# A decoder layer on one core: cross-attention queries of six of eight head groups as seven block products for eight

## The chip, the cores and the metric

One core of a Trainium2 chip runs the whole kernel. The metric is the time of one execution on the device, in microseconds (us); a kernel is run several times and the median is given. A profiled execution is one further run with the hardware profiler on; its span reaches from the first to the last instruction.

## The reference

One post-norm decoder layer in float32, on 8 sequences of 128 tokens with 512 features: x = LN(x + SelfAttention(x)); x = LN(x + CrossAttention(x, ctx)); x = LN(x + FeedForward(x)). What matters here is the cross-attention:

```
q = (query @ wq), 32 heads of 128, rotated by position     k, v = key @ wk, value @ wv, 8 heads of 128
rotate(t) = t * cos + concat(-t[64:], t[:64]) * sin
out = softmax(q k^T / sqrt(128) + mask) v,  heads 4g to 4g+3 use key head g;   result = out @ wo
```

wq is 512 x 4096. With the tokens of all sequences side by side, a head's query tile is a 128 x 1024 product with a contraction of 512.

## The kernel before, in words

Every matmul operand is split into an upper and a lower half (fp32r), and a product is three passes of them: `product`, line 31, whose matmuls all carry line L35. The program is a chain of four classes: ProjectSelf, AttendSelf, AttendCross (prefix C_ in the rows), FeedForward (D_). Each engine's instructions are written out by hand in one order, and semaphores are waited for one by one; an instruction that waits holds up all behind it on its engine.

AttendCross works through 64 steps, step n for head group n // 8 and sequence n % 8, plus three steps to drain. In a step (`decoder_layer`, from line 1750) TensorE does, in this order: the transposes of the probabilities of step n - 2 (`transpose`, L1096), the scores of step n (`scores`, L1114), the output product of step n - 3 (`outputs`, twelve matmuls with wo), the values of step n - 2 (`values`, three matmuls with C_pT), and one query tile (`queries`, `project`), twelve matmuls: four chunks of the contraction by three passes, 128 features of one head by 512 tokens. Five tiles ahead of their use, one a step, until step 58.

VectorE in a step (`vector`, from L1217): the reciprocal of step n - 1's sums (L1190); the rotation of a query tile (`rotate`, L1165 to L1167: the cosine on 128 partitions, the sine on two halves of 64, as the halves change places), read from the PSUM bank of the product; the lower half of the transposed probabilities of step n - 2 (`turned_lo`, L1196), which the value products wait for; the masked row minima (L1180); the residual (L1228); the lower half of the head outputs (`output_lo`, L1203).

ScalarE: upper half of the transposes (L1046), upper half of the outputs (L1055, waits for the values), four exponentials (L1035), and the upper half of one piece of weights (`Ring.hi`, L166). GpSimd (`gpsimd`, from L1244): softmax scaling of step n - 1 (L1249), which waits for the reciprocal; the rotation's sum (`tile_sum`, L1242); the lower half of one piece of weights (`Ring.lo`, L171), which waits for ScalarE's.

Weights come in pieces of 128 x 512 through a ring of five slots (`Ring`, line 140); a load waits until the piece five before it is split. SP issues all DMAs, in order: in `AttendCross.sync` (L1006) the pieces, and between them the keys and values of a whole group (1.5 MB, two buffers). Scores and transposes have two PSUM banks each, the query products two.

Of the kernel before, what the change touches and what calls it, by code (L numbers as in the profile page):

```python
# [5 lines left out]
F32 = mybir.dt.float32  # L6
F32R = mybir.dt.float32r
# [4 lines left out]
P = 128  # L12
# [11 lines left out]
KV = 3 * NT  # L24
# [432 lines left out]
class AttendSelf:  # L457
# [80 lines left out]
    def sync(self, eng):  # L538
# [3 lines left out]
        for n in range(self.STEPS):  # L542
# [29 lines left out]
            if n == self.NS + 1:  # L572
# [4 lines left out]
                self.cross.load_kv(eng, 0)  # L577
# [353 lines left out]
class AttendCross:  # L931
# [3 lines left out]

    Q = HG
# [5 lines left out]
    STEPS = NS + 3  # L942

    def __init__(self, chip, before, x1, trig, rows, ring, first, kv_d, dram):
# [7 lines left out]
        self.kv = [pool(f"kv{i}", (36, 16)[i], [P, KV], F32R) for i in range(2)]  # L952
        self.q = [pool(f"q{half}", 104 + 8 * half, [P, self.Q, HALF]) for half in range(2)]
# [21 lines left out]

    def query(self, r):

        return by_batch(self.q[r // self.Q % 2][:, r % self.Q, :])

    def split(self, n):  # L980


        piece = 2 * self.Q * (n // B + 1) + n % B - 1
        return piece if 2 * self.Q <= piece < self.PIECES else None

    def target(self, i):

        g, j = i // (2 * self.Q), i % (2 * self.Q)
        return [t[:, :] for t in (self.w[j] if j < self.Q else self.wo[g % 2][j - self.Q])]


    def load_piece(self, eng, i):

        src = self.dram["wq" if i % (2 * self.Q) < self.Q else "wo"][i // (2 * self.Q), :, i % self.Q, :]
        self.ring.load(eng, self.first + i, src)

    def load_kv(self, eng, g):

        wait(eng, self.s_pv, B * (g - 1))
        eng.dma_start(self.kv[g % 2][:, :].bitcast(F32), self.kv_d[g]).then_inc(self.s_kv[g % 2], 16)  # L1000
# [5 lines left out]
    def sync(self, eng):  # L1006
# [5 lines left out]
        self.load_kv(eng, 1)  # L1012
# [845 lines left out]
```

## Time and profile before

| | |
|---|---|
| median of 3 runs (881.39 to 882.78) | 881.53 us |
| the profiled execution | 884.05 us |
| its span | 881.9 us |
| TensorE clock granted over the span | 0.997 of full |

A row of a view with lines reads: line, engine, operation, output<-inputs by the program's names, count, then busy time, mean of one, idle time before. A row in order of time reads: start, duration, engine, line, operation, count, and in brackets the idle time before it and what ended it. PE is TensorE's matmul queue, PEld its weight loads, DVE is VectorE, ACT ScalarE, POOL GpSimd.

### The profile page before, as it was taken

The page shows a single profiled execution, that of the slowest core. Times are in us where ns is not written, and L with a number is a line of the kernel's source. Part 1 is how long each engine was busy: PE and PEld are TensorE (multiplying, and loading weights), DVE is VectorE, ACT ScalarE, POOL GpSimd, SP SyncE. Part 2 cuts the span into 40 slices and gives each one's busy share as a digit, 9 for nine tenths or more (in the row PEclk, how much of TensorE's full clock was granted, in tenths as well). Part 3 has the DMA queues.
Part 4 walks back from the last instruction along what each step waited for, and adds up shares of the span by engine and source line. Part 5 has one row for each costly group of instructions (what it writes and reads, how often), then busy time and mean ns, then how long its engine had stood idle before and what let it go on. Part 6 is the DMA issues. An engine that isn't in the chain of part 4 may idle for free.

```text
span 881.9 us, 15308 instructions
## 1 busy us (share of the span) xinstructions
PE 855.9 (97%) x4748; PEld 708.9 (80%) x4748; DVE 604.5 (69%) x2030; ACT 425.8 (48%) x1424; POOL 455.0 (52%) x406
## 2 busy tenths in 40 slices
PE   7999899999999999999999999999999999999996
PEld 6787788788877788888888888888888887778884
DVE  5466688788877676766766666666666767545646
ACT  5336877777771544444444444444444446341320
POOL 4726766766675544444444444444444578545102
PEclk9999999999999999999999999999999999999998
DMA  8679987876864111211212112013131123000001
GB/s 294 261 218 202 217 187 162 182 152 153 162 206 177 37 36 37 108 37 65 80 36 108 37 34 102 34 37 108 37 107 37 49 69 100 13 25 25 25 1 48
DMA packets 68368, 88.23 MB, mean 100 GB/s; under 512 B 7232, under 2 KB 44352, under 8 KB 67264
## 3 DMA queue, kind: packets, MB, share of 16 engines
q1 hardware_dynamic: 68288, 87.26, 36.0%
q8 instruction: 39, 0.64, 0.3%
q14 instruction: 41, 0.34, 0.2%
HBM read 64.13 MB, written 23.07 MB: 99 GB/s over the span
## 4 chain that ended last, share of the span: by engine, by line
PE 85%; DVE 4%; POOL 3%; issue 3%; DMA 3%; ACT 2%; SPq 1%; POOLq 0%; ACTq 0%; DVEq 0%
PE banks L35 67%; PE banks L1114 6%; PE banks L1096 3%; PE banks L752 3%; PE banks L770 2%; PE banks L743 1%; DMA heads_k<-heads_k_d 1%; DMA stage<-wv_dram 1%; POOL B_wv L171 1%; SPq L213 1%; PE banks L367 1%; PE banks L122 1%; POOL x L114 0%; ACT B_prob L681 0%; POOL D_up L171 0%
## 5 line engine op out<-in xcount | busy, mean ns | idle before, releaser
L35 PE MATMUL banks<-C_wo,C_o 128*128 128x512 f32 x768 | 192.3, 399 | 0.8 <-issue 0.5
L35 PE MATMUL banks<-xT,C_w 128*128 128x512 f32 x768 | 185.7, 390 | 0.8 <-DVE xT L137 0.8
L35 PEld LDWEIGHTS banks<-xT,C_w 128*128 128x128 f32 x768 | 143.6, 188 | 31.1 <-issue 1.6
L35 PEld LDWEIGHTS banks<-C_wo,C_o 128*128 128x128 f32 x768 | 139.6, 188 | 28.9 <-issue 1.3
L1055 ACT ACTIVATE C_o<-banks 128x512 fp32r<-128x512 f32 x64 | 38.3, 598 | 227.7 <-PE banks L35 227.7
L681 ACT ACTIVATE B_prob<-B_prob,B_top 128x128 f32<-128x128 f32 x256 | 99.5, 392 | 27.6 <-DVE B_top L838 27.5
L1035 ACT ACTIVATE C_prob<-C_prob,C_top 128x128 f32<-128x128 f32 x256 | 99.0, 391 | 10.1 <-DVE C_top L1180 10.1
L171 POOL TENSOR_TENSOR C_wo<-stage,C_wo 128x512 fp32r<-128x512 f32 x32 | 40.9, 1277 | 110.6 <-ACT C_wo L166 110.6
L171 POOL TENSOR_TENSOR C_w<-stage,C_w 128x512 fp32r<-128x512 f32 x32 | 40.8, 1276 | 101.9 <-ACT C_w L166 101.8
L1242 POOL TENSOR_TENSOR C_q<-C_t,C_t 128x512 f32<-128x512 f32 x64 | 82.8, 1294 | 16.1 <-DVE C_t L1167 16.1
L593 POOL TENSOR_TENSOR B_prob<-B_prob,B_rden 128x512 f32<-128x512 f32 x64 | 67.6, 1056 | 40.3 <-DVE B_rden L847 40.1
L1203 DVE TENSOR_TENSOR C_o<-banks,C_o 128x512 fp32r<-128x512 f32 x64 | 44.2, 691 | 41.6 <-ACT C_o L1055 41.6
L1249 POOL TENSOR_TENSOR C_prob<-C_prob,C_rden 128x512 f32<-128x512 f32 x64 | 66.4, 1037 | 10.7 <-DVE C_rden L1190 10.7
L838 DVE CUSTOM_DVE_ANT_0 B_prob<-banks,causal 128x128 f32<-128x128 f32 x256 | 58.9, 286 | 17.1 <-issue 15.5
L1114 PE MATMUL banks<-C_kv,C_q 128*128 128x128 f32 x512 | 67.6, 275 | 0.0
L1228 DVE TENSOR_TENSOR x<-banks,x 128x512 f32<-128x512 f32 x64 | 44.2, 691 | 27.1 <-PE banks L35 27.1
L1114 PEld LDWEIGHTS banks<-C_kv,C_q 128*128 128x128 f32 x512 | 62.4, 192 | 0.2
L1165 DVE TENSOR_TENSOR C_t<-banks,trig 128x512 f32<-128x512 f32 x64 | 44.2, 690 | 24.4 <-PE banks L35 24.4
L1180 DVE CUSTOM_DVE_ANT_0 C_prob<-banks,C_mask 128x128 f32<-128x128 f32 x256 | 58.9, 286 | 0.6 <-issue 0.5
L35 PE MATMUL banks<-C_pT,C_kv 128*128 128x512 f32 x192 | 54.5, 392 | 2.6 <-issue 2.4
L1046 ACT ACTIVATE C_pT<-banks 128x512 fp32r<-128x512 f32 x64 | 38.1, 595 | 30.8 <-PE banks L1096 30.8
L35 PE MATMUL banks<-cT,B_wk 128*128 128x512 f32 x192 | 52.0, 406 | 0.4 <-DVE B_t L904 0.4
(150 smaller groups left out, 1636.6 us busy)
## 6 DMA issues: line engine op xcount, KB each, us to landing
C_kv<-cross_kv_d SPq DMA_DIRECT2D x8, 1536.0 KB, 7.1
cross_kv_d<-B_v_out SPq DMA_DIRECT2D x16, 512.0 KB, 4.7
stage<-wq_dram SPq DMA_DIRECT2D x32, 256.0 KB, 2.6
stage<-wo_dram SPq DMA_DIRECT2D x32, 256.0 KB, 2.6
heads_q<-heads_q_d SPq DMA_DIRECT2D x96, 64.0 KB, 3.6
heads_k<-heads_k_d SPq DMA_DIRECT2D x96, 64.0 KB, 3.8
heads_q_d<-cT SPq DMA_DIRECT2D x8, 512.0 KB, 2.9
heads_k_d<-cT SPq DMA_DIRECT2D x8, 512.0 KB, 2.8
```

The lines of the kernel that those rows point to most:

```text
L35: mm = eng.matmul(out, stationary[i], moving[j], start=first and n == 0, stop=last and n == len(PASSES) - 1)
L171: eng.tensor_tensor(out, self.stage[:, self.slot(n), :], hi.bitcast(F32), ALU.subtract).then_inc(self.s_lo, 1)
L593: eng.tensor_tensor(e, e, self.rden[:, m % 2, :].unsqueeze(2).broadcast_to([P, HG, S]), ALU.mult).then_inc(self.s_norm, 1)
L681: last = eng.activation(e, e, ACT.Exp, bias=self.top[:, n % 4, h:h + 1], scale=-1.0, accum_out=self.total[:, n % 2, h:h + 1])
L838: last = eng.tensor_tensor_reduce(self.prob[:, n % 4, h * S:(h + 1) * S], self.sc[n % 2][:, h * S:(h + 1) * S], self.heads.causal, 1.0, 3e ...
L1035: last = eng.activation(e, e, ACT.Exp, bias=self.top[:, n % 2, h:h + 1], scale=-1.0, accum_out=self.total[:, n % 2, h:h + 1])
L1114: mm = eng.matmul(self.sc[n % 2][:, h * S:(h + 1) * S], self.q[s // 4][:, h, tok], keys, start=True, stop=True)
L1165: eng.tensor_tensor(by_batch(t1), by_batch(bank), cos, ALU.mult).then_inc(self.s_cos, 1)
L1180: last = eng.tensor_tensor_reduce(self.prob[:, n % 2, h * S:(h + 1) * S], self.sc[n % 2][:, h * S:(h + 1) * S], self.mask[:, n % B, :], 1. ...
L1203: eng.tensor_tensor(self.o[1][:, :], self.ov, self.o[0][:, :].bitcast(F32), ALU.subtract).then_inc(self.s_olo, 1)
L1242: eng.tensor_tensor(self.query(r), by_batch(t1), by_batch(t2), ALU.add).then_inc(self.s_sum, 1)
L1249: eng.tensor_tensor(e, e, self.rden[:, (n - 1) % 2, :].unsqueeze(2).broadcast_to([P, self.Q, S]), ALU.mult).then_inc(self.s_norm, 1)
```

## The change

Head groups 0 and 1 are computed as before. For groups 2 to 7, twelve pairs of heads, the four query tiles of a pair (two heads by two halves of the tokens) come from seven block products in place of eight (Winograd's form of Strassen's scheme): the blocks are the two halves of the contraction. A block product is two chunks by three passes, six matmuls of 512 columns.

- Pair k is multiplied in steps 7 + 4k to 10 + 4k (`multiplying`, phases 0 to 3) with 12, 9, 9 and 12 matmuls, and its weight blocks are made in the four steps before (`preparing`): four sums of 256-column blocks and seven lower halves on GpSimd, seven upper halves on ScalarE, where four pieces were split in two halves each; two wo pieces a pair are split as before, in phases 0 and 1.
- The tokens' sums are made once, in steps 3 to 8, on VectorE (`token_sums`, 24 instructions with two SBUF operands, at the end of the step), with their upper halves on ScalarE.
- The products are added up: five additions a pair on VectorE (a PSUM bank and an SBUF tile), two on GpSimd, two copies to SBUF on ScalarE. A tile is rotated in steps 10 + 4k to 13 + 4k; the rotation reads the tile from SBUF (t1 or h), the sine first, then, after a wait, the cosine.
- Steps 3 to 6 make two plain tiles each (groups 0 and 1), steps 4 to 7 rotate two.
- Scores and transposes have one bank each, as four banks go to the products. Keys and values come in 64 loads of one step in five slots. k is stored with 512-byte rows for it.
- FeedForward's first pieces are split two steps earlier.

The core of the diff:

```diff
+    def preparing(self, n):
+        k, phase = divmod(n - self.AT + 4, 4)
+        return (k, phase) if 0 <= k < self.PAIRS else (None, 0)
+    def multiplying(self, n):
+        k, phase = divmod(n - self.AT, 4)
+        return (k, phase) if 0 <= k < self.PAIRS else (None, 0)
...
+    def blocks_hi(self, eng, n):
...
+            for i in range(2):
+                done = eng.activation(self.block(k, i, 0), a[:, 256 * i:256 * i + 256].rearrange("p (c n) -> p c n", c=2),
+                                      ACT.Copy)
+                done.then_inc(self.ring.s_hi if i else self.s_bhi, 1)
+            for i in range(2, 4):
+                self.sum_hi(eng, k, i)
...
+    def copy_products(self, eng, n):
+        k, phase = self.multiplying(n)
+        if k is None:
+            return
+        if phase == 0:
+            eng.wait_ge(self.s_st, 7 * k + 1)
+            wait(eng, self.s_u, 3 * (k - 1) + 1)
+            if k == 0:
+                eng.wait_ge(self.s_t, self.T_RAW[3, 1])
+            eng.activation(self.p1[:, :], self.alpha, ACT.Copy).then_inc(self.s_p1, 1)
+        if phase == 2:
+            eng.wait_ge(self.s_st, 7 * k + 5)
+            if k > 0:
+                eng.wait_ge(self.s_cos, self.PLAIN + 4 * k)
+                eng.wait_ge(self.s_sin, self.PLAIN + 4 * k)
+            eng.activation(self.h[:, :], self.gamma, ACT.Copy).then_inc(self.s_p7, 1)
...
+            wait(eng, self.s_phi, n - 2)
+            wait(eng, self.s_plo, n - 2)
...
+            wait(eng, self.s_top, n)
...
+        if n < self.AT:
+            self.project(eng, 2 * n + 2)
+            self.project(eng, 2 * n + 3)
+        k, phase = self.multiplying(n)
+        if k is None:
+            return
+        x = lambda half, inner: [self.rows.xT[:, 4 * half:4 * half + 4, lo, 2 * inner:2 * inner + 2, :] for lo in range(2)]
+        t = lambda i: [self.T[i][:, lo, :, :] for lo in range(2)]
+        if phase == 0:
+            wait(eng, self.s_e, k)
+            self.block_product(eng, k, 0, self.alpha, x(0, 0), (True, True))
+            wait(eng, self.s_u, 3 * (k - 1) + 1)
+            self.block_product(eng, k, 1, self.beta, x(0, 1), (True, True))
+        if phase == 1:
+            if k == 0:
+                eng.wait_ge(self.s_Tlo, 4)
+                eng.wait_ge(self.s_sin, self.PLAIN)
+            eng.wait_ge(self.s_p1, k + 1)
+            self.block_product(eng, k, 2, self.alpha, t(2), (True, True))
+            wait(eng, self.s_u, 3 * k)
+            self.block_product(eng, k, 3, self.delta, t(1), (True, False), (0,))
+        if phase == 2:
+            if k == 0:
+                eng.wait_ge(self.s_Tlo, 6)
+            self.block_product(eng, k, 3, self.delta, t(1), (False, True), (1,))
+            wait(eng, self.s_u, 3 * (k - 1) + 2)
+            self.block_product(eng, k, 4, self.gamma, x(1, 0), (True, True))
+        if phase == 3:
+            if k == 0:
+                eng.wait_ge(self.s_Tlo, 8)
+            eng.wait_ge(self.s_p5, k + 1)
+            self.block_product(eng, k, 5, self.delta, x(1, 1), (True, True))
+            eng.wait_ge(self.s_p7, k + 1)
+            self.block_product(eng, k, 6, self.gamma, t(4), (True, True))
...
+        t1 = self.t1[:, r % 2, :]
+        if r < self.PLAIN:
+            eng.wait_ge(self.s_pj, r + 1)
+            wait(eng, self.s_sum, r - 1)
+            self.times_cos(eng, r, self.pj[r % 2])
+            self.times_sin(eng, r, self.pj[r % 2])
+        else:
+            wait(eng, self.s_sum, r - 1)
+            src = self.tile_from_products(eng, r, t1)
+            self.times_sin(eng, r, src)
+            eng.wait_ge(self.s_sin, r + 1)
+            self.times_cos(eng, r, src)
+    def times_cos(self, eng, r, src):
+        cos = self.trig[:, 0, :].unsqueeze(1).broadcast_to([P, 4, S])
+        eng.tensor_tensor(by_batch(self.t1[:, r % 2, :]), by_batch(src), cos, ALU.mult).then_inc(self.s_cos, 1)
+    def times_sin(self, eng, r, src):
+        t2, sin = self.t2[:, r % 2, :], self.trig[:, 1, :].unsqueeze(1).broadcast_to([P, 4, S])
+        eng.tensor_tensor(by_batch(t2[0:64, :]), by_batch(src[64:128, :]), sin[0:64], ALU.mult)
+        eng.tensor_tensor(by_batch(t2[64:128, :]), by_batch(src[0:64, :]), sin[64:128], ALU.mult).then_inc(self.s_sin, 1)
...
+    def add_products(self, eng, n):
+        k, phase = self.multiplying(n)
+        if k is None:
+            return
+        if phase == 1:
+            eng.wait_ge(self.s_p1, k + 1)
+            eng.wait_ge(self.s_st, 7 * k + 3)
+            wait(eng, self.s_u, 3 * k)
+            wait(eng, self.s_h2, k)
+            eng.tensor_tensor(self.e[:, :], self.alpha, self.p1[:, :], ALU.add).then_inc(self.s_e, 1)
+        if phase == 2:
+            eng.wait_ge(self.s_e, k + 1)
+            eng.wait_ge(self.s_st, 7 * k + 4)
+            eng.tensor_tensor(self.p5[:, :], self.delta, self.e[:, :], ALU.add).then_inc(self.s_p5, 1)
...
+    def tile_from_products(self, eng, r, t1):
+        k, i = self.pair(r)
+        if i == 3:
+            eng.wait_ge(self.s_h2, k + 1)
+            return self.h[:, :]
+        eng.wait_ge(self.s_st, 7 * k + (2, 7, 6)[i])
+        if i == 0:
+            eng.wait_ge(self.s_p1, k + 1)
+        elif i == 1:
+            eng.wait_ge(self.s_h1, k + 1)
+        else:
+            eng.wait_ge(self.s_p5, k + 1)
+        eng.tensor_tensor(t1, (self.beta, self.gamma, self.delta)[i], (self.p1, self.e, self.p5)[i][:, :], ALU.add)\
+           .then_inc(self.s_u, 1)
+        eng.wait_ge(self.s_u, 3 * k + i + 1)
+        return t1
...
+        self.add_products(eng, n - 1)
+        tiles = self.tiles(n)
+        for r in tiles[:1]:
+            self.rotate(eng, r)
         self.turned_lo(eng, n - 2)
...
+        for r in tiles[1:]:
+            self.rotate(eng, r)
+        self.token_sums(eng, n)
...
+        k, phase = self.multiplying(n - 1)
+        if k is not None and phase == 2:
+            eng.wait_ge(self.s_p5, k + 1)
+            eng.wait_ge(self.s_p7, k + 1)
+            eng.tensor_tensor(self.e[:, :], self.e[:, :], self.h[:, :], ALU.add).then_inc(self.s_h1, 1)
+            eng.wait_ge(self.s_h1, k + 1)
+            eng.tensor_tensor(self.h[:, :], self.h[:, :], self.p5[:, :], ALU.add).then_inc(self.s_h2, 1)
+        self.blocks_lo(eng, n)
...
+            eng.tensor_tensor(S1, b[:, 0:256], b[:, 256:512], ALU.add).then_inc(self.s_raw, 1)
+            eng.wait_ge(self.s_raw, 4 * k + 1)
+            eng.tensor_tensor(S2, S1, a[:, 0:256], ALU.subtract).then_inc(self.s_raw, 1)
+            eng.tensor_tensor(S3, a[:, 0:256], b[:, 0:256], ALU.subtract).then_inc(self.s_raw, 1)
+            eng.wait_ge(self.s_raw, 4 * k + 2)
+            eng.tensor_tensor(S4, a[:, 256:512], S2, ALU.subtract).then_inc(self.s_raw, 1)
...
+        if phase == 2:
+            for i in range(2):
+                eng.wait_ge(self.ring.s_hi if i else self.s_bhi, self.staged(k, 0)[1] + 1 if i else 5 * k + 1)
+                self.block_lo(eng, k, i, a[:, 256 * i:256 * i + 256])
+        if phase >= 2:
+            eng.wait_ge(self.s_raw, 4 * k + 4)
+            for i in range(2 * phase - 2, 2 * phase):
+                eng.wait_ge(self.s_bhi, 5 * k + i)
+                self.block_lo(eng, k, i, self.raw_block(k, i))
+        if phase == 3:
+            eng.wait_ge(self.ring.s_hi, self.staged(k, 1)[1] + 1)
+            self.block_lo(eng, k, 6, b[:, 256:512])
...
-    SPLIT = {57: (0, 1), 58: (2, 3), 59: (4, 5), 60: (6, 7), 61: (8, 9), 62: (10, 11), 63: (12,)}
+    SPLIT = {55: (0, 1), 56: (2, 3), 57: (4, 5), 58: (6, 7), 59: (8, 9), 60: (10, 11), 61: (12,)}
```

## Rows read from the trace of the kernel before

**Rows 1.** The page's first part: busy us, share of the span, instructions.

```profile
PE 855.9 (97%) x4748; PEld 708.9 (80%) x4748; DVE 604.5 (69%) x2030; ACT 425.8 (48%) x1424; POOL 455.0 (52%) x406
```

**Rows 2.** Busy time by stretch, mid cross-attention: stretch, length, engines, clock, DMA, GB/s.

```profile
460.00:700.00 240.00, 240.00 (x1250) 203.41 (x1249) 165.66 (x513) 104.50 (x354) 113.57 (x97) 1.00 0.18 62
```

**Rows 3.** TensorE in order of time, one step of the cross-attention.

```profile
559.93 0.84 PE L35 MATMUL banks<-C_pT,C_kv 128*128 128x512 f32 x3
560.61 2.88 PE L35 MATMUL banks<-xT,C_w 128*128 128x512 f32 x12
563.33 0.60 PE L1096 MATMUL banks<-ident,C_prob 128*128 128x128 f32 x4
563.77 1.06 PE L1114 MATMUL banks<-C_kv,C_q 128*128 128x128 f32 x8
564.58 3.00 PE L35 MATMUL banks<-C_wo,C_o 128*128 128x512 f32 x12
567.42 0.84 PE L35 MATMUL banks<-C_pT,C_kv 128*128 128x512 f32 x3
```

**Rows 4.** VectorE in order of time, the same step.

```profile
562.98 0.18 DVE L1190 RECIPROCAL C_rden<-C_total 128x4 f32<-128x4 f32 x1 [0.84 <-ACT C_prob L1035]
563.53 0.69 DVE L1165 TENSOR_TENSOR C_t<-banks,trig 128x512 f32<-128x512 f32 x1 [0.38 <-PE banks L35]
564.25 0.69 DVE L1166 TENSOR_TENSOR C_t<-banks,trig 64x512 f32<-64x512 f32 x1
564.96 0.68 DVE L1167 TENSOR_TENSOR C_t<-banks,trig 64x512 f32<-64x512 f32 x1
565.68 0.69 DVE L1196 TENSOR_TENSOR C_pT<-banks,C_pT 128x512 fp32r<-128x512 f32 x1
```

**Rows 5.** ScalarE in order of time, the same step.

```profile
562.46 0.39 ACT L1035 ACTIVATE C_prob<-C_prob,C_top 128x128 f32<-128x128 f32 x1
...
562.84 0.62 ACT L166 ACTIVATE C_wo<-stage 128x512 fp32r<-128x512 f32 x1
```

**Rows 6.** GpSimd in order of time, the same step.

```profile
563.54 1.28 POOL L171 TENSOR_TENSOR C_wo<-stage,C_wo 128x512 fp32r<-128x512 f32 x1 [3.96 <-ACT C_wo L166]
564.78 1.04 POOL L1249 TENSOR_TENSOR C_prob<-C_prob,C_rden 128x512 f32<-128x512 f32 x1
565.79 1.29 POOL L1242 TENSOR_TENSOR C_q<-C_t,C_t 128x512 f32<-128x512 f32 x1
```

**Rows 7.** VectorE in order of time, two SBUF operands, beside GpSimd.

```profile
18.82 1.36 DVE L390 TENSOR_TENSOR A_xT<-A_rest,A_xT 128x512 fp32r<-128x512 f32 x1 [1.22 <-ACT A_xT L325]
...
791.83 1.43 DVE L1576 TENSOR_TENSOR D_hT<-D_sq,D_hT 128x512 fp32r<-128x512 f32 x1 [0.27 <-ACT D_hT L1376]
```

**Rows 8.** GpSimd in order of time, at the same two moments.

```profile
18.35 1.29 POOL L430 TENSOR_TENSOR cT<-A_val,cT 128x512 fp32r<-128x512 f32 x1 [5.65 <-ACT cT L335]
...
791.35 1.36 POOL L171 TENSOR_TENSOR D_down<-stage,D_down 128x512 fp32r<-128x512 f32 x1 [1.95 <-ACT D_down L166]
```

**Rows 9.** One GpSimd line: least/median/most ns, first and last start.

```profile
L1694 POOL TENSOR_TENSOR x<-x,D_beta x8: 1273/1288/1733, 792.7 to 802.3; 128x512 f32<-128x512 f32 x8
```

**Rows 10.** VectorE in order of time, two SBUF operands, GpSimd only clearing memory.

```profile
5.24 0.69 DVE L390 TENSOR_TENSOR A_w<-stage,A_w 128x512 fp32r<-128x512 f32 x1
5.88 0.69 DVE L390 TENSOR_TENSOR A_xT<-stage,A_xT 128x512 fp32r<-128x512 f32 x1
```

**Rows 11.** GpSimd in order of time, its narrowest two-operand instruction.

```profile
11.71 0.25 POOL L442 TENSOR_TENSOR A_flat_hl<-A_flat,A_flat_hl 128x32 fp32r<-128x32 f32 x1
```

**Rows 12.** VectorE in order of time, a step without queries or rotation.

```profile
735.13 0.17 DVE L1190 RECIPROCAL C_rden<-C_total 128x4 f32<-128x4 f32 x1
735.22 0.66 DVE L1196 TENSOR_TENSOR C_pT<-banks,C_pT 128x512 fp32r<-128x512 f32 x1
```

**Rows 13.** TensorE in order of time, the value products of two such steps.

```profile
735.98 0.93 PE L35 MATMUL banks<-C_pT,C_kv 128*128 128x512 f32 x3
...
741.53 0.93 PE L35 MATMUL banks<-C_pT,C_kv 128*128 128x512 f32 x3
```

More of the change, by code:

```diff
@@ L23 @@
 EPS = 1e-5
-KV = 3 * NT
+KV = 3 * P
 VW = 3 * DH * HS // 2
@@ L992, in load_piece @@
-    def load_piece(self, eng, i):
[L994 to L1000, printed above, removed]
+        half, j = r // self.Q, r % self.Q
+        if r >= self.PLAIN:
+            k, i = self.pair(r)
+            half, j = 2 * (k // 2 + 2) + i // 2, 2 * (k % 2) + i % 2
@@ new lines, in splits, with block, raw_block @@
+    def splits(self, n):
+        if n in self.SPLIT:
+            return self.SPLIT[n]
+        k, phase = self.preparing(n)
+        return (12 + 4 * k + phase,) if k is not None and phase < 2 else ()
+    def target(self, i):
+        kind, g, j = self.ORDER[i]
+        return [t[:, :] for t in (self.w[j] if kind == "wq" else self.wo[g % 2][j])]
+    def block(self, k, i, lo):
+        return self.blocks[(7 * k + i) % len(self.blocks)][:, lo, :, :]
+    def raw_block(self, k, i):
+        return self.block_sums[(7 * k + i) % len(self.blocks)][:, 1, :]
@@ new lines, in staged, with wait_staged, T_part @@
+    def staged(self, k, second):
+        n = self.first + 14 + 4 * k + second
+        return self.ring.stage[:, self.ring.slot(n), :], n
+    def wait_staged(self, eng, k):
+        for second in range(2):
+            n = self.staged(k, second)[1]
+            eng.wait_ge(self.ring.s_piece[self.ring.slot(n)], 16 * (n // self.ring.SLOTS + 1))
+    def T_part(self, i, lo, c):
+        if i == 3:
+            return self.rows.xT[:, 4:8, lo, c, :]
+        return by_batch(self.T[i][:, lo, c, :])
@@ new lines, in queries, with block_product @@
+        if phase == 3:
[5 more added lines that the diff above has]
+            self.block_product(eng, k, 6, self.gamma, t(4), (True, True))
+    def block_product(self, eng, k, i, bank, moved, ends, chunks=(0, 1)):
+        if i in (1, 6):
+            eng.wait_ge(self.ring.s_lo, self.staged(k, i == 6)[1] + 1)
+        else:
+            eng.wait_ge(self.s_block, 5 * k + max(i, 1))
+        for c in chunks:
+            mv = [t[:, c, :] if len(t.shape) == 3 else t[:, :, c, :] for t in moved]
+            mm = product(eng, bank, [self.block(k, i, lo)[:, c, :] for lo in range(2)], mv, ends[0] and c == 0,
+                         ends[1] and c == 1)
+        if 1 in chunks:
+            mm.then_inc(self.s_st, 1)
```

256 lines of the change are left out of this document (186 added, 70 removed).

## The prediction

> **What bounds the kernel now.** I read the busy shares first, then the busy time by stretch, then the order of time of one step of the cross-attention, engine by engine, and last every VectorE instruction elsewhere in the trace that reads two SBUF operands. TensorE is busy 97% of the span, and VectorE and GpSimd only 69% and 52% [rows 1]. In the 240 us in the middle of the cross-attention TensorE is busy for all 240.00 [rows 2]. So the step costs what TensorE's work costs, and one of its instructions saved is time saved, as long as nothing else takes its place.
>
> I count a step from V, the end of the three value products. One ends at 559.93 + 0.84 = 560.77, the next at 567.42 + 0.84 = 568.26, so a step is 7.49 us [rows 3]. From V on TensorE runs twelve query matmuls, the transposes, the scores, twelve output matmuls and the next three value matmuls. Twelve query matmuls take 563.33 - 560.61 = 2.72 us from start to start, 0.227 each.
>
> The value products read the lower half of the transposed probabilities, L1196 on VectorE. It ends at 566.37, and the products start at 567.42 [rows 3, 4]: **the slack is 1.05 us**. VectorE's chain there starts with the reciprocal at V + 2.21, held by ScalarE's exponentials, which follow V themselves. Then come three rotation instructions 0.72 apart, then L1196. This is a loop from V to the next V that TensorE's own work hides today by one microsecond only. What the change puts between the reciprocal and L1196 is therefore the first thing to price.
>
> **What goes.** Each of twelve pairs of heads does seven products of six matmuls for eight: 12 x 6 x 0.227 = 16.3 us of TensorE. The four steps of a pair would fall from 4 x 7.49 = 29.96 to 28.60 us: two with twelve query matmuls (7.49) and two with nine (6.81). Loads, scores, outputs and values stay. The queries of steps 55 to 58 move to steps 3 to 6; TensorE's total doesn't change by that. A step without queries is 7.49 - 2.72 = 4.77 us. In the steps without queries today the three value products end 5.55 us apart where other stages' work is in them too [rows 12, 13]. So these four steps cost between 0 and 4 x 0.78 = 3.1 us. I take 0, since the loop without a rotation is shorter than 4.77: reciprocal at 2.21, the next instruction 0.09 after its start, 0.66, then 1.03 to the end of the values (735.88 to 736.91) [rows 12, 13].
>
> **What comes on VectorE.** Per pair five additions of a product bank and an SBUF tile (0.69 each, like L1196 [rows 4]): one, the error sum or the fifth product, ahead of the rotation in two steps, and one inside the rotation in three. That is 2 x 0.69 ahead of L1196 in step 3 of the pair (0 to 3, the diff's phase), 0.69 in the other three.
>
> **The rotation changes form.** Today it reads a PSUM bank and the table, and L1165 took 0.69 with GpSimd's L171 running through it [rows 4, 6]: no contention. After the change its three instructions read t1 or h and the table, both in SBUF. What such an instruction does beside GpSimd is shown elsewhere. L390 began at 18.82 while GpSimd's L430 ran until 18.35 + 1.29 = 19.64, and ended at 20.18; L1576 began at 791.83 with L171 running until 792.71, and ended at 793.26 [rows 7, 8]. Alone it takes 0.69 [rows 10]. So it waits until the GpSimd instruction has ended, and needs 0.55 from there. The reverse holds too: L1694, 1.288 at the median, took 1.733 at its longest, 0.45 more [rows 9]. The two engines take turns.
>
> **GpSimd's order in the new step.** In-order: leftovers of the step before, the softmax scaling (1.04), the rotation's sum (waits for the rotation; 1.29), the rest. ScalarE splits weights after the exponentials, until V + 2.69 [rows 5], so the matching GpSimd half comes at V + 2.77 to 4.05, as today [rows 6], and the scaling behind it. Both fall into the rotation. A 256-column GpSimd instruction isn't in the trace. From 0.25 for 32 columns [rows 11] and 1.28 for 512 I estimate 0.73, and 0.42 for a 256-column ScalarE copy between 0.39 and 0.62 [rows 5].
>
> Step by step, from V, with VectorE's first instruction at 2.30:
> - **Steps 1 and 2.** Addition 2.30 to 2.99. First sine half at 3.03, waits for L171 to 4.05, ends 4.60. The scaling, held back, runs to 5.50; second half ends 6.05. GpSimd now waits for the rotation, so the cosine is free: 6.10 to 6.79. L1196 ends 7.51, values 1.03 later: 8.54 each, where TensorE needs 7.49 and 6.81.
> - **Step 3.** Two additions to 3.63, sine at 3.67. ScalarE makes four block halves from 2.1 on, so GpSimd has four 0.73 instructions from about 2.5 and then the scaling. Sine halves end 4.50 and 5.75, the cosine 6.95, L1196 7.67, values 8.70.
> - **Step 0.** The addition waits for the last query matmul, V + 2.72, and ends 3.46. GpSimd still has the two 512-column sums of the products (until about V + 3.3) and three block halves. Ends: 4.60, 5.80, 7.00, L1196 7.70, values 8.73.
>
> Sum 8.73 + 8.54 + 8.54 + 8.70 = 34.5 per pair, 4.55 over 29.96; twelve pairs: **+54.6 us**, TensorE's saving already in it.
>
> The unknown in this is the order of turns, which no row shows for two such VectorE instructions in a row. I bound it by three cases. GpSimd takes every turn: +54.6. VectorE goes on with the second half and loses only the turn at the cosine, which waits for a semaphore: 8.4, 8.4, 8.1, 8.2, sum 33.1, +38. GpSimd never gets in between: 7.55, 7.55, 7.6, 7.65, sum 30.35, +5. I take the first, because rotation instructions start 0.03 after the one before has ended, where in stage A two of one partition range start 0.64 apart and overlap [rows 4, 10]: in that gap nothing of VectorE's stands in the way of a waiting GpSimd instruction.
>
> The Trainium skill, VectorE: DVE Perf Modes, section Two Vector instructions with no wait between them, says that an instruction whose input starts in another quadrant than the last one read starts only when all before it have finished. By that rule the second sine half can't hold the turn and the sum is the first case; without it, the second. The spacings of 0.72 and 0.64 agree with it; that GpSimd gets in is shown by no run yet.
>
> **The start.** Steps 3 to 8 carry 24 token sums and splits on VectorE, all with two SBUF operands, behind the step's last instruction, and steps 4 to 7 two rotations each. TensorE's steps 3 to 6 grow to 7.49 + 2.72 = 10.21. VectorE's own step is 165.66 / 32 = 5.2 us today [rows 2], and with a second rotation (2.1) and four sums (2.8) 10.1: about covered. Step 7 has six and a second rotation, 5.2 + 2.1 + 4.1 = 11.4 us in a step of 7.49, and if each of the six waits half a GpSimd instruction, 15.2; step 8 follows with four more. Between 0 (VectorE's idle third takes it all up) and 12 us (7.7 in step 7, 4 in the others); I take the middle, 6.
>
> **Costed at nothing.** ScalarE's split blocks and product copies (at most 2.2 us a step) lie behind the exponentials, and its copy of the transposes is needed only when VectorE reaches L1196; without that cover 0.6 each. The single score and transpose banks wait for work that ended a step earlier. The smaller key and value loads are asked for three steps ahead; SP's queue waits there on the values and on the split pieces of the same step, and the next loads queue behind that, over two steps early. Product waits on TensorE (block halves, the three product copies) are met a step ahead.
>
> Total: 884.05, the profiled execution, + 54.6 + 6 = 944.6. That execution lies 2.5 over the median of the runs, 881.53. **Forecast 942 us.**
>
> **Rivals.**
> 1. *GpSimd seldom in the way* (third case; +5 and 0 to 12 for the start): about 893, 884 to 915. For it: GpSimd idles while the rotation runs, as its sum waits for it. Against: leftovers and scaling sit exactly at V + 2.8 to 5.
> 2. *The other side: the turns don't bind and the loop shrinks under TensorE.* Then step 2 is 6.90 and step 3 7.56, the other two 7.49: 29.44, -0.52 a pair, -6 in all; with a start near 2 us, 877. If VectorE's whole chain stays covered, -16.3: 865 to 871. The price is the wait of the three rotation instructions; it decides where they wait together less than 0.2 us a step (7.76 + 7.10 + 7.58 + 7.49 = 29.93). Against: both L390 and L1576 waited to the last.
> 3. *No net change*: saving and waits cancel, which needs waits of just about 0.2 us a step and a free start.
>
> **How the numbers follow.** A difference of 0.2% (1.8 us) is about what can be told here. Forecast, either order of turns with waits, 915 to 955: 0.66. Rival 1: 0.14. Rival 3: 0.05. Rival 2: 0.11. Over 955 (a start worse than bounded): 0.04. The range 884 to 955 holds the first two, 0.80. Slower 0.66 + 0.14 + 0.04 = 0.84.
>
> **What would show it.** Right: query matmuls 768 less 72; steps 8.5 to 8.7 us between 7 and 54; TensorE idle ahead of the value products, some 70 us, released by L1196's successor on VectorE; the first sine half near 1.5 us and the cosine 0.7 in steps 1 and 2; softmax scaling near 1.5 instead of 1.04. Wrong: rotation instructions at 0.7, TensorE still without gaps in the middle, steps of 6.8 to 7.5.

## The result, and the profile after

| | before | after |
|---|---|---|
| median | 881.46 us (880.90 to 882.78, 4 runs) | 937.07 us (936.25 to 937.78, 4 runs) |
| span of the profiled execution | 881.9 us | 934.5 us |
| ratio | | 1.0622, 95% interval 1.0604 to 1.064 |

The change makes the kernel 6.2% slower. The forecast was 942 us, with 884 to 955 as its range.

The page's first part answers to [rows 1]: TensorE has 72 matmuls fewer, 4676 for 4748, and falls from 97% of the span to 92%; VectorE goes from 69% to 77%, GpSimd from 52% to 64%.

```profile
PE 856.7 (92%) x4676; PEld 693.1 (74%) x4676; DVE 721.5 (77%) x2114; ACT 451.8 (48%) x1516; POOL 596.1 (64%) x538
```

Busy time by stretch of the kernel after. The columns are those of [rows 2], the third row its stretch. The first row holds steps 3 to 9, from one V (the end of the value products) to another, the second steps 10 to 57. In [rows 2] TensorE was busy for all 240.00 us; now it is idle for 27.2 of them.

```profile
286.85:360.31 73.46, 63.87 (x307) 51.28 (x306) 68.44 (x148) 29.16 (x92) 47.47 (x40) 0.98 0.17 55
360.31:760.49 400.18, 352.06 (x1781) 283.85 (x1781) 338.39 (x828) 178.57 (x610) 298.53 (x266) 1.00 0.18 57
460.00:700.00 240.00, 212.83 (x1077) 172.02 (x1078) 202.87 (x499) 107.84 (x372) 180.56 (x164) 1.00 0.18 55
```

The same two stretches of the kernel before, cut at its own V's: 52.36 and 359.84 us.

```profile
291.00:343.36 52.36, 50.27 (x263) 42.26 (x261) 38.06 (x117) 22.63 (x77) 27.28 (x23) 1.00 0.12 41
343.36:703.20 359.84, 359.84 (x1873) 304.95 (x1873) 248.36 (x769) 157.05 (x530) 171.37 (x145) 1.00 0.18 62
```

TensorE in order of time, one step of the kernel after (step 25, nine query matmuls, phase 2), answers to [rows 3]. The value products now stand idle for 1.35 us first. The profile puts that wait down to "issue"; what ends just ahead of them is L1493 on VectorE, at 492.88 + 0.68 = 493.56.

```profile
485.26 0.93 PE L35 MATMUL banks<-C_pT,C_kv 128*128 128x512 f32 x3 [0.64 <-issue]
486.03 2.21 PE L35 MATMUL banks<-C_T,C_block 128*128 128x512 f32 x9
...
489.32 3.00 PE L35 MATMUL banks<-C_wo,C_o 128*128 128x512 f32 x12
493.67 0.93 PE L35 MATMUL banks<-C_pT,C_kv 128*128 128x512 f32 x3 [1.35 <-issue]
```

VectorE in the same step, against [rows 4]: the reciprocal, one addition, the rotation in three instructions (now sine, sine, cosine), and L1493, which was L1196.

```profile
488.40 0.18 DVE L1487 RECIPROCAL C_rden<-C_total 128x4 f32<-128x4 f32 x1 [0.84 <-ACT C_prob L1143]
488.57 0.69 DVE L1404 TENSOR_TENSOR C_e<-banks,C_p 128x512 f32<-128x512 f32 x1
489.30 1.49 DVE L1390 TENSOR_TENSOR C_t<-C_h,trig 64x512 f32<-64x512 f32 x1
490.80 1.44 DVE L1391 TENSOR_TENSOR C_t<-C_h,trig 64x512 f32<-64x512 f32 x1
492.28 0.69 DVE L1385 TENSOR_TENSOR C_t<-C_h,trig 128x512 f32<-128x512 f32 x1
492.88 0.68 DVE L1493 TENSOR_TENSOR C_pT<-banks,C_pT 128x512 fp32r<-128x512 f32 x1
```

GpSimd in the same step, against [rows 6].

```profile
488.96 1.28 POOL L171 TENSOR_TENSOR C_wo<-stage,C_wo 128x512 fp32r<-128x512 f32 x1 [0.15 <-ACT C_wo L166]
490.20 1.49 POOL L1554 TENSOR_TENSOR C_prob<-C_prob,C_rden 128x512 f32<-128x512 f32 x1
493.05 1.28 POOL L1547 TENSOR_TENSOR C_q<-C_t,C_t 128x512 f32<-128x512 f32 x1 [1.35 <-DVE C_t L1385]
```

Here one can read off how the two engines take turns. The weight piece runs until 490.24; the first sine half, waiting since 489.30, ends 0.55 us later, at 490.79. The softmax scaling has waited since 490.20 and takes the next turn, until 491.69; the second half ends 0.55 us after that, at 492.24. Then GpSimd has to wait for the rotation itself, and the cosine is free, 0.69. It is so throughout: between 285 and 770 us of this trace 131 VectorE instructions with two SBUF operands take more than 0.75 us, and in each of them one GpSimd instruction, never two, ends 0.54 to 0.55 us before VectorE's own end.

Groups of instructions of the kernel after, with the mean of one and the idle time before. The rotation's three instructions, 0.68 to 0.69 us each in [rows 4], now take 0.95 to 1.44 in the mean of a group (0.69 to 1.55 singly); the scaling takes 1.371 for 1.04 in [rows 6]; TensorE is idle for 55.7 us before its value products.

```profile
L35 PE MATMUL banks<-C_pT,C_kv 128*128 128x512 f32 x192 | 59.8, 420 | 55.7 <-issue 55.5
...
L1391 DVE TENSOR_TENSOR C_t<-C_t,trig 64x512 f32<-64x512 f32 x36 | 44.4, 1234 | 0.5
L1390 DVE TENSOR_TENSOR C_t<-C_t,trig 64x512 f32<-64x512 f32 x36 | 39.2, 1088 | 1.2
L1385 DVE TENSOR_TENSOR C_t<-C_t,trig 128x512 f32<-128x512 f32 x36 | 34.1, 948 | 1.2
L1391 DVE TENSOR_TENSOR C_t<-C_h,trig 64x512 f32<-64x512 f32 x12 | 17.3, 1438 | 0.2
...
L1554 POOL TENSOR_TENSOR C_prob<-C_prob,C_rden 128x512 f32<-128x512 f32 x64 | 87.8, 1371 | 19.3 <-DVE C_rden L1487 19.3
```

The 52.6 us between the spans, stage by stage (a step n reaches from the V of n - 1 to its own):

| stretch | before | after | difference |
|---|---|---|---|
| up to V of step 2 | 291.00 | 286.85 | -4.2 |
| steps 3 to 9 | 52.36 | 73.46 | +21.1 |
| steps 10 to 57 | 359.84 | 400.18 | +40.3 |
| steps 58, 59 | 14.99 | 10.26 | -4.7 |

Of the +21.1, 4 x 2.72 = 10.9 us are the query matmuls that moved there; 10.2 are a stall. The profiled execution before lies 2.5 us above its median (884.05 for 881.53) and the one after 0.8 below (936.25 for 937.07), so that the spans differ by 3 us less than the medians, 55.6.

### The profile page after: what moved, and what is told of

Its sections match the earlier page's. It is cut to its first block, busy times and chain, and to the rows that moved or that the text cites. A ratio compares the mean times of both kernels' runs of the same rounds, so it can differ in the third digit from the quotient of the medians.

```text
span 934.5 us, 15753 instructions
## 1 busy us (share of the span) xinstructions
PE 856.7 (92%) x4676; PEld 693.1 (74%) x4676; DVE 721.5 (77%) x2114; ACT 451.8 (48%) x1516; POOL 596.1 (64%) x538
## 4 chain that ended last, share of the span: by engine, by line
PE 81%; issue 9%; DVE 5%; ACT 2%; POOL 1%; DMA 1%; POOLq 0%; DVEq 0%; ACTq 0%
PE banks L35 64%; PE banks L1277 6%; PE banks L1260 3%; PE banks L752 3%; PE banks L770 2%; PE banks L743 1%; DMA stage<-wv_dram 1%; ACT B_prob L681 1%; PE banks L122 1%; POOL B_wv L171 1%; PE banks L367 1%; DVE B_prob L838 0%; PE banks L370 0%; PE banks L371 0%; DVE C_t L1385 0%
## 5 line engine op out<-in xcount | busy, mean ns | idle before, releaser
L35 PE MATMUL banks<-C_pT,C_kv 128*128 128x512 f32 x192 | 59.8, 420 | 55.7 <-issue 55.5
L1143 ACT ACTIVATE C_prob<-C_prob,C_top 128x128 f32<-128x128 f32 x256 | 99.1, 391 | 10.2 <-DVE C_top L1477 10.2
L1554 POOL TENSOR_TENSOR C_prob<-C_prob,C_rden 128x512 f32<-128x512 f32 x64 | 87.8, 1371 | 19.3 <-DVE C_rden L1487 19.3
L35 PEld LDWEIGHTS banks<-C_pT,C_kv 128*128 128x128 f32 x192 | 31.9, 190 | 81.3 <-issue 78.0
L35 PE MATMUL banks<-xT,C_block 128*128 128x512 f32 x288 | 71.7, 391 | 0.0
L171 POOL TENSOR_TENSOR C_wo<-stage,C_wo 128x512 fp32r<-128x512 f32 x32 | 42.4, 1326 | 33.8 <-ACT C_wo L166 33.1
L35 PEld LDWEIGHTS banks<-xT,C_block 128*128 128x128 f32 x288 | 54.1, 188 | 11.9
L35 PE MATMUL banks<-C_T,C_block 128*128 128x512 f32 x216 | 56.0, 395 | 0.0
L2064 POOL TENSOR_TENSOR D_rstd<-D_moments,power 128x1 f32<-128x1 f32 x16 | 11.9, 742 | 63.5 <-DVE D_moments L1961 63.5
L1610 POOL TENSOR_TENSOR C_block<-stage,C_block 128x256 fp32r<-128x256 f32 x36 | 31.9, 900 | 32.1 <-ACT C_block L1192 32.1
```

Of the source, the lines that this page charges most:

```text
L35: mm = eng.matmul(out, stationary[i], moving[j], start=first and n == 0, stop=last and n == len(PASSES) - 1)
L171: eng.tensor_tensor(out, self.stage[:, self.slot(n), :], hi.bitcast(F32), ALU.subtract).then_inc(self.s_lo, 1)
L1143: last = eng.activation(e, e, ACT.Exp, bias=self.top[:, n % 2, h:h + 1], scale=-1.0, accum_out=self.total[:, n % 2, h:h + 1])
L1554: eng.tensor_tensor(e, e, self.rden[:, (n - 1) % 2, :].unsqueeze(2).broadcast_to([P, self.Q, S]), ALU.mult).then_inc(self.s_norm, 1)
```

## The experiments

All kernels below are the kernel after with one edit or a few, except e4. Line numbers shift by some lines between them; the names tell which instruction is which. The kernel before, measured beside each set, had medians of 881.5 (e1 to e4), 881.4 (e5 to e7) and 880.8 us (e9, e10).

### e1: the sums stay in PSUM

```diff
...
-        eng.tensor_tensor(t1, (self.beta, self.gamma, self.delta)[i], (self.p1, self.e, self.p5)[i][:, :], ALU.add)\
-           .then_inc(self.s_u, 1)
+        bank = (self.beta, self.gamma, self.delta)[i]
+        eng.tensor_tensor(bank, bank, (self.p1, self.e, self.p5)[i][:, :], ALU.add).then_inc(self.s_u, 1)
         eng.wait_ge(self.s_u, 3 * k + i + 1)
-        return t1
+        return bank
```

The block products that reuse a bank wait for the rotation in place of the addition, and the cosine's wait for the sine is kept for the fourth tile alone, which stays in SBUF (C_h).

> The sum of product and correction goes back into the product's PSUM bank, so three of the four tiles of a pair are rotated from PSUM again; the fourth still reads h in SBUF. Instruction counts are the same. Theory (turns with GpSimd on two SBUF operands cost the time): the rotation's instructions go back to 0.7 us in phases 3, 0 and 1, these steps fall from 8.46, 8.31 and 8.40 to about 7.6, 7.5 and 7.5 us, phase 2 stays at 8.4: 31.0 for 33.6 a pair, 12 x 2.6 = 31 us, so about 906. Rival (the five added instructions make VectorE's chain too long by themselves): steps stay at 8.2 or more, over 930.

905.08 us (one run). Steps of phase 3, 0 and 1 take 7.36, 7.50 and 7.51 us, the one that rotates C_h (phase 2) 8.41 as before the edit. Groups of instructions of e1:

```profile
L1397 DVE TENSOR_TENSOR C_t<-banks,trig 64x512 f32<-64x512 f32 x52 | 36.0, 693 | 1.7
...
L1397 DVE TENSOR_TENSOR C_t<-C_h,trig 64x512 f32<-64x512 f32 x12 | 17.1, 1426 | 0.4
```

The same multiplication by the same table takes 0.693 us from a PSUM bank and 1.426 from SBUF, GpSimd's work being the same. This one edit gives back 32 us, as its theory expected (906), and steps 10 to 57 fall from 400.18 to 367.05.

### e2: the softmax scaling behind the rotation's sum

```diff
+        if n >= self.AT:
+            for r in self.tiles(n):
+                self.tile_sum(eng, r)
         if self.live(n, 1):
             eng.wait_ge(self.s_rden, n)
...
-        for r in self.tiles(n):
-            self.tile_sum(eng, r)
+        if n < self.AT:
+            for r in self.tiles(n):
+                self.tile_sum(eng, r)
```

> GpSimd does the rotation's sum ahead of the softmax scaling in steps 7 to 64, so the scaling can't come between the two sine halves. Theory (each turn is lost to a GpSimd instruction that stands ready): in phases 1 and 2 the second sine half falls from 1.44 to 0.7 us and the steps from 8.40 to about 7.6; phases 3 and 0, where block halves take the turns, keep 8.4: 12 x 1.6 = 19 us, about 918. Rival (VectorE waits for the first GpSimd instruction only and then runs on; the second half is long for another reason): no change, 937.

928.04 us (one run): 9 us for the 19 expected. Phase 1 came out as expected, 7.65 us, phase 2 did not, 8.25, and phase 0 takes 8.50 for 8.31. VectorE of e2 in a phase 1 step, then in the phase 2 step behind it:

```profile
479.98 1.55 DVE L1390 TENSOR_TENSOR C_t<-C_t,trig 64x512 f32<-64x512 f32 x1
481.54 0.69 DVE L1391 TENSOR_TENSOR C_t<-C_t,trig 64x512 f32<-64x512 f32 x1
...
487.71 1.06 DVE L1390 TENSOR_TENSOR C_t<-C_h,trig 64x512 f32<-64x512 f32 x1
488.78 1.69 DVE L1391 TENSOR_TENSOR C_t<-C_h,trig 64x512 f32<-64x512 f32 x1
```

GpSimd of e2 over the same two steps:

```profile
479.71 1.28 POOL L171 TENSOR_TENSOR C_wo<-stage,C_wo 128x512 fp32r<-128x512 f32 x1 [2.05 <-ACT C_wo L166]
...
487.49 0.74 POOL L1596 TENSOR_TENSOR C_block_sum<-stage,C_block_sum 128x256 f32<-128x256 f32 x1
488.17 1.75 POOL L171 TENSOR_TENSOR C_wo<-stage,C_wo 128x512 fp32r<-128x512 f32 x1
```

In phase 1 the first half still waits for the weight piece; behind that GpSimd has nothing left that can run, and the second half takes 0.69. In phase 2 the scaling's move pushed the four block sums and the piece into the rotation, and the piece takes the turn between the two halves. So the turn goes to whichever GpSimd instruction is ready, the scaling or another. The rival, a second half that is long for another reason, is out by phase 1.

### e3: the rotation behind the minima

```diff
-        for r in tiles[:1]:
+        late = tiles[:1] if n >= self.AT else ()
+        for r in tiles[:1] if n < self.AT else ():
             self.rotate(eng, r)
         self.turned_lo(eng, n - 2)
         self.minima(eng, n)
+        for r in late:
+            self.rotate(eng, r)
```

> From step 7 on VectorE rotates behind the lower half of the transposes and the minima; contention is left as it is. Theory (the rotation costs because the value products wait behind it): TensorE's idle time ahead of the value products goes, steps fall to 7.5 us or a little less, 12 x 3.6 = 43 us, about 894; the rotation's instructions are free to stay long. Rival (VectorE with its waits for GpSimd is the bound by its total): steps of 8.2 and more, over 925.

897.13 us (one run) for about 894 expected. Steps 10 to 57 take 353.75 us, 6.1 below the kernel before, although single rotation instructions still take up to 1.69 us: off the way to the values contention costs much less, though it is not free. Three of four steps are TensorE's own 6.8, 6.8 and 7.5; the fourth (phase 1) takes 8.0 or, every second time, 9.0. TensorE of e3 in such a step:

```profile
470.54 0.66 PE L1260 MATMUL banks<-ident,C_prob 128*128 128x128 f32 x4 [0.43 <-POOL C_prob L1557]
471.76 1.16 PE L1277 MATMUL banks<-C_kv,C_q 128*128 128x128 f32 x8 [0.57 <-POOL C_q L1550]
```

GpSimd of e3 just ahead:

```profile
469.44 1.04 POOL L1557 TENSOR_TENSOR C_prob<-C_prob,C_rden 128x512 f32<-128x512 f32 x1
470.44 1.26 POOL L1550 TENSOR_TENSOR C_q<-C_t,C_t 128x512 f32<-128x512 f32 x1
```

The transposes wait for a scaling that ends at 470.48, and in the first step of a group the scores wait for the rotation's sum as well. GpSimd's own block halves ahead of these lost turns to the rotation (1.20 us each for 0.73 to 0.74), so it is late. That this alone makes the long steps was only argued here; e5 bears it out.

### e4: the layout of keys and values alone, in the kernel before

```diff
-                eng.dma_start(self.kv_d[j // 2][:, j % 2 * HALF:(j % 2 + 1) * HALF],
-                              self.k_out[j % 2][:, :, :].rearrange("p b s -> p (b s)")).then_inc(self.s_kout[j % 2], 16)
+                eng.dma_start(self.kv_d[j // 2][:, 4 * (j % 2):4 * (j % 2) + 4, 0:S], self.k_out[j % 2][:, :, :])\
+                   .then_inc(self.s_kout[j % 2], 16)
...
```

> The kernel before with only the layout of keys and values in DRAM of the change (k stored in 512-byte rows by sequence; the loads stay whole groups). In the changed kernel the self-attention's steps 3 to 8 were 4.2 us shorter. Theory A (the layout does it): 877, with the same 4 us gained in those steps. Theory B (the landing of those loads varies from run to run): 881.5, as before.

The values and the loads follow the same layout. 881.86 us (880.36 to 886.72, 10 runs), ratio 1.0012, interval 0.9994 to 1.0031: no gain. The V of step 2 lay at 287.58 here, at 290.04 in e3, which has the new layout too, at 286.81 to 286.89 in after, e1, e2, e5 and e7, and at 288.50 to 289.71 in e6, e9 and e10. Up to there all of these but e4 have the same instructions as after, and still this point moves by 3.2 us, so the 4.2 us of the table's first row are not shown to be the change's.

### e5: e1 and e3 together

> Both e1's and e3's edits: the sums stay in PSUM, and the rotation stands behind the minima. Theory A (what the changed kernel lost in steps 10 to 57 is the contended rotation inside the loop from the reciprocal to L1196, nothing else): TensorE sets every step, two of 7.5 and two of 6.8 us a pair, 343 us for steps 10 to 57 against 353.75 in e3 and 359.84 before; the extra of the start stays; 885 to 888 us. Theory B (another engine is the bound by now, GpSimd's order for instance): no better than e3, 897, with the 8.0 and 9.0 us steps of e3 still there. A middle case: only every second of these steps stays long, since the scores of the first step of a group wait for a tile that was rotated in the step before; then about 893.

880.01 us (879.11 to 881.31, 8 runs), ratio 0.9978, interval 0.9959 to 0.9996; better than the 885 to 888 of theory A. Steps 10 to 55 are 6.8, 7.5, 7.5 and 6.8 us throughout, with none of e3's long steps. Busy time by stretch of e5, steps 10 to 57:

```profile
360.18:701.35 341.17, 339.46 (x1781) 287.25 (x1780) 289.97 (x825) 178.54 (x610) 264.96 (x264) 1.00 0.21 67
```

In steps 10 to 55 the product's whole saving is now there, and over steps 10 to 57 TensorE is busy for 339.46 of 341.17 us. Steps 3 to 9 are as they were, 73.37 us.

### e6, e7, e9: the start

VectorE of the kernel after between the V's of steps 5 and 6, to show what the start loses: the second rotation and four token sums stand at the end of a step, and behind them come the next reciprocal, the next rotation and L1493.

```profile
319.07 0.68 DVE L1385 TENSOR_TENSOR C_t<-banks,trig 128x512 f32<-128x512 f32 x1
...
321.81 1.78 DVE L1450 TENSOR_TENSOR C_T_sum<-xT 128x512 f32<-128x512 f32 x1
323.52 1.22 DVE L1449 TENSOR_TENSOR C_T_sum<-C_x,C_T_sum 128x512 f32<-128x512 f32 x1
324.67 1.21 DVE L1450 TENSOR_TENSOR C_T_sum<-xT 128x512 f32<-128x512 f32 x1
...
327.99 0.69 DVE L1493 TENSOR_TENSOR C_pT<-banks,C_pT 128x512 fp32r<-128x512 f32 x1
```

GpSimd beside them makes lower halves of blocks, 0.73 to 0.75 us each where nothing is in the way; two of them:

```profile
323.01 2.32 POOL L1610 TENSOR_TENSOR C_block<-stage,C_block 128x256 fp32r<-128x256 f32 x2
```

TensorE waits there twice: its second query product for the second rotation, which still holds the bank, and its value products for L1493.

```profile
321.32 3.01 PE L35 MATMUL banks<-xT,C_w 128*128 128x512 f32 x12 [0.78 <-DVE C_t L1391]
...
328.79 0.94 PE L35 MATMUL banks<-C_pT,C_kv 128*128 128x512 f32 x3 [0.36 <-issue]
```

The largest wait is in step 8. The second rotation and six token instructions of step 7 stand ahead of its L1493, the last four of them here, and the value products stand idle for 3.26 us. TensorE's clock falls behind that: from 351.90 to 359.00 us it was granted 0.84 of the full clock in the mean. VectorE and TensorE of the kernel after:

```profile
346.75 3.58 DVE L1463 TENSOR_TENSOR C_T<-C_T_sum,C_T 128x512 fp32r<-128x512 f32 x4
```

```profile
351.10 1.62 PE L35 MATMUL banks<-C_pT,C_kv 128*128 128x512 f32 x3 [3.26 <-issue]
352.52 3.03 PE L35 MATMUL banks<-C_T,C_block 128*128 128x512 f32 x9
```

In the step shown first, the same matmuls take 0.93 and 2.21 us, so the lower clock costs 1.5 us here.

e6 changes the order on VectorE and GpSimd, and on ScalarE (first hunk) that of the upper halves which this needs:

```diff
-        for i in {6: (1, 2), 7: (3, 4)}.get(n, ()):
+        for i in {5: (1,), 6: (2,), 7: (3, 4)}.get(n, ()):
...
-        for i in {7: (1, 2), 8: (3, 4)}.get(n, ()):
+        for i in {6: (1,), 7: (2,), 8: (3, 4)}.get(n, ()):
...
-        for r in tiles[:1]:
+        first = tiles[:1] if n > self.AT else tiles
+        for r in first:
             self.rotate(eng, r)
         self.turned_lo(eng, n - 2)
         self.minima(eng, n)
+        self.token_sums(eng, n)
...
-        for r in tiles[1:]:
-            self.rotate(eng, r)
-        self.token_sums(eng, n)
...
+        if n < self.AT:
+            self.blocks_lo(eng, n)
         for r in self.tiles(n):
             self.tile_sum(eng, r)
...
-        self.blocks_lo(eng, n)
+        if n >= self.AT:
+            self.blocks_lo(eng, n)
```

> Only the order of steps 3 to 8 is changed: both rotations first, the token sums ahead of the residual instead of at the end, two lower halves of the token sums in step 6 instead of 7, GpSimd's block halves ahead of its rotation sums until step 6. Theory A (the start is lost because sums and second rotation stand in VectorE's order ahead of L1493): steps 4 to 8 fall from 11.3 to 11.9 us to 10.2 to 10.9, steps 3 to 9 from 73.5 to 66 to 68 us, the kernel to 930 to 932 us. Theory B (the sums' contention with GpSimd itself is the loss, wherever they stand): steps 3 to 9 stay at 72 to 74 us, 936 to 938.

938.08 us (2 runs): no gain, steps 3 to 9 at 72.82. But the reason is not theory B alone. VectorE of e6: the four token sums of step 5 now take 0.68 to 0.69 each, GpSimd being idle beside them, and a new wait stands in their place.

```profile
322.00 0.68 DVE L1450 TENSOR_TENSOR C_T_sum<-xT 128x512 f32<-128x512 f32 x1
...
327.88 0.69 DVE L1385 TENSOR_TENSOR C_t<-banks,trig 128x512 f32<-128x512 f32 x1 [3.91 <-POOL C_q L1545]
```

The rotation waits until GpSimd has summed an earlier tile out of the same buffer, and e6 had put the block halves, which wait for ScalarE, ahead of that sum.

e7 is e1's edit, e6's, and e3's from step 8 on in all steps but the last of each group:

> Sums in PSUM, start in e6's order, rotation behind the minima except in the last step of each group, where the next step's scores need its tile. Theory A (contended instructions on VectorE's way to the values are all that the change lost): TensorE sets all steps, the kernel comes out under the one before, 873 to 879 us. Theory B (the start or the steps keep a second bound): 882 to 890.

888.26 us (885.67 to 890.17, 10 runs), ratio 1.0076, interval 1.0057 to 1.0094: worse than e5. e6's start is in it (73.37), and the exception costs too: the last step of a group takes 9.08 us. VectorE of e7 there:

```profile
459.16 0.70 DVE L1431 TENSOR_TENSOR banks<-banks,C_e 128x512 f32<-128x512 f32 x1 [1.46 <-POOL C_e L1572]
```

With the rotation early, its addition waits for GpSimd's sum of two products, which stands behind the rotation sum of the step before, late there.

e9 is e6 without the last two hunks of its diff, GpSimd's:

> e6 without its edit on GpSimd: the rotation sums stay ahead of the block halves, as in the changed kernel; on VectorE both rotations first, the token sums ahead of the residual, two lower halves in step 6 instead of 7. Theory A (e6 only replaced one wait by another: rotations waited for the rotation sums, which stood behind the block halves): steps 4 to 8 take 10.2 to 10.9 us and the eighth 7.5, steps 3 to 9 65 to 68 us, the kernel 929 to 932 us. Theory B (sums and rotations cost the start the same wherever they stand): steps 3 to 9 at 72 to 74 us, 936 to 938.

933.36 us (2 runs). Steps 6, 7 and 8 now are TensorE's, 10.23, 10.21 and 7.52 us, where they were 11.93, 11.30 and 11.70; steps 4 and 5 stay long, 12.60 and 11.77. Steps 3 to 9 take 67.45 for 73.46:

```profile
289.71:357.16 67.45, 62.77 (x308) 51.92 (x306) 61.38 (x148) 28.84 (x92) 43.92 (x40) 0.97 0.19 60
```

So theory A holds for 6 of the 10.2 us. The rest fits theory B, though no run takes it away: in steps 4 and 5 the sums still meet GpSimd and stand ahead of the rotations. VectorE of e9 ahead of the values of step 4, with one of the four sums, and of step 5:

```profile
297.47 1.78 DVE L1440 TENSOR_TENSOR C_x<-xT 128x512 f32<-128x512 f32 x1
...
309.32 1.17 DVE L1443 TENSOR_TENSOR C_T_sum<-C_x,C_T_sum 128x512 f32<-128x512 f32 x1
```

The medians differ by 3.7 us and not by 6; in the profile of e9 the V of step 2 lies at 289.71, 2.9 later than in after.

### e10: e1, e3 and e9 together

e3's order holds from step 8 on.

> e5 with e9's order of the start. Theory A: e5's time less what e9 gives back, 872 to 876 us, below the kernel before in every pair of runs. Theory B: the start stays, 879 to 881.

874.26 us (872.93 to 874.84, 6 runs) against 880.80 (11 runs) beside it: ratio 0.9915, interval 0.9895 to 0.9935. This is the fastest version, as theory A expected (872 to 876). Steps 3 to 9 take 67.13 us. Busy time of e10 in steps 10 to 57:

```profile
355.69:696.83 341.14, 339.40 (x1780) 287.20 (x1779) 289.76 (x825) 178.49 (x610) 265.01 (x264) 1.00 0.21 67
```

## Why the prediction was right, point by point

**The mechanism, and the order of turns: right.** The first sine half at 1.49, the cosine at 0.69 and the scaling at 1.49 are what the text gave for steps 1 and 2. The second half's 1.44 is the first of its three bound cases, GpSimd taking every turn. e1 shows that the source in SBUF is the cause, e2 that it needs a GpSimd instruction ready at that moment, e3 and e5 that nearly all of the cost comes from its place ahead of L1493. Rivals 1 to 3 all needed rotation waits that are small; they are out.

The Trainium skill, VectorE: DVE Perf Modes, section Two Vector instructions with no wait between them, by which the second sine half must wait for the first to finish, gave the first case too. The trace agrees: the second half starts 0.01 us after the first has ended, and GpSimd has got in between. But the reason that the prediction gave for the first case, the gap of 0.03 us between rotation instructions, is not what decides it. The token sums shown under the start have no such gap: 323.52 comes 0.07 us before the sum ahead has ended (321.81 + 1.78 = 323.59), and 324.67 likewise. GpSimd gets in between all the same, and they take 1.22 and 1.21 us. The case was right, the argument for it not needed.

**The length of the steps: forecast 0.9 us a pair too long.** Phases 0 to 3, forecast 8.73, 8.54, 8.54, 8.70 (34.5), measured 8.31, 8.40, 8.41, 8.46 (33.6), all below the 8.5 to 8.7 that were to show it right. In the phase 2 step shown above the rotation's three instructions end at V + 4.60, 6.05 and 6.78, as reckoned to 0.01 us; L1493 then starts 0.60 us after the cosine's start, which is 0.09 before the cosine ends, where the sum had it wait for the end. In phases 0 and 3 GpSimd's block halves of 256 columns leave shorter waits than the sum had; in phase 0 the sine halves take 0.81 and 1.14, the cosine 1.11. For steps 10 to 55 this makes 386.2 us against 414 - 8.54 - 8.54 = 396.9, -10.7.

**The queries moved to the start: a slip.** "TensorE's total doesn't change by that" is true, but steps 56 and 57, which lose their queries, still rotate the last pair's tiles, so their loop, not TensorE, sets them. They take 14.0 us, where the sum had 17.08 - 2 x 2.72 = 11.6: +2.4. The two steps behind them take 10.26 for 14.99 - 5.44 = 9.55: +0.7, inside the bound of 3.1 for the four.

**The start: 10.2 us measured where the sum had 6, inside its bounds of 0 and 12, +4.2.** The term that was mis-sized is the token sums: they take up to 1.8 us instead of 0.69, and they stand ahead of the next L1493. The sum had looked at whether VectorE has time for them, not at what is queued behind them, and so had steps 4 to 7 as about covered. These take 11.66, 11.94, 11.93 and 11.30 us for TensorE's 10.21, 6.0 in all, where the sum's upper bound had 4 outside step 7; step 8, behind step 7's six, takes 11.70 for 7.49, +4.2, where the bound had 7.7. Two things were not foreseen: the second query product's wait for the second rotation, 0.8 us in each of three steps, and the lower clock behind step 8's wait, 1.5 us. e9 took 6.0 us away by order alone, 4.2 of them in step 8.

**The stage before: -4.2 us,** not forecast, and not shown to be the change's (e4). Some 3 us of it may be the two executions that were profiled, as their spans differ by 52.6 us and the medians by 55.6.

Together -10.7 + 2.4 + 0.7 + 4.2 - 4.2 = -7.6, against 934.5 - (881.9 + 60.6) = -8.0 in the spans. Between the medians the forecast of 942 is 4.9 us too high. That closeness is partly luck: errors of 10.7 one way and 7.3 the other stand against each other.

**Costed at nothing: right.** No wait of TensorE on block halves, product copies or the single banks of scores and transposes shows in the kernel after. TensorE's idle time ahead of the value products, forecast as some 70, is 55.7; the steps are shorter than forecast.

## What to carry to other kernels

Before work is added to an engine, look at what is queued behind it and who waits for that: here a saving of 16 us on the busiest engine made the kernel 55.6 us slower, and the same arithmetic in another order and another memory (additions kept in PSUM, the rotation behind what the values wait for, the start in e9's order) is 6.5 us faster than before. On VectorE, an instruction with two SBUF operands is priced by what GpSimd has ready at that moment, not by its own 0.69 us. A change of order moves waits as readily as it removes them (e6, e7), so read after each one what is late next.

## What was not expected of the hardware

The two engines alternate where both have something ready, in all 131 long VectorE instructions of the kernel after: a waiting scaling got its turn between two sine halves, the second of which starts 0.01 us after the first has ended, and in e2 a weight piece did. GpSimd pays as well, 0.45 us for the scaling (1.49 for 1.04) and 0.47 for a weight piece (L171 1.28 in after, 1.75 in e2), and through this its own queue gets late, which in e3 reached TensorE.

TensorE's clock was not in the forecast. In the kernel after it costs 1.5 us behind step 8's wait, as shown above. In e9 the value products of step 4 stand idle for 1.97 us, and the stretch behind them was granted 0.76 of the full clock (2.4 GHz) in the mean, part of it at half; its 24 query matmuls take 7.21 us, where those of the next step take 5.61. Busy time of that stretch of e9, and the matmuls in order of time:

```profile
309.40:316.50 7.10, 7.10 (x25) 5.63 (x24) 7.07 (x9) 2.65 (x10) 6.64 (x6) 0.76 0.14 44
```

```profile
309.46 7.21 PE L35 MATMUL banks<-xT,C_w 128*128 128x512 f32 x24
...
321.27 5.61 PE L35 MATMUL banks<-xT,C_w 128*128 128x512 f32 x24
```

It cost little there: in e10, with 1.96 us of idle time ahead and the full clock behind it, the step takes 11.56 us for e9's 11.77, as VectorE's sums set both. So a wait of this length is not followed by the lower clock every time.
